# Top-k experts in two groups of two batches, the selection moved beside attention and beside the experts

## The chip, the cores and the metric

The kernel runs as one program on one core of a Trainium2 chip. A core has five engines with instruction queues of their own: TensorE (PE in the profile; its weight loads are PEld), VectorE (DVE), ScalarE (ACT), GpSimd (POOL) and SyncE (SP, which only issues transfers here). They meet through semaphores. The metric is the device time in microseconds of one execution. Before the change the median of three runs is 1038.39 us (1035.84 to 1040.92).

## The reference

Four batches of 512 tokens with 256 columns pass through two layers. Each layer is a cross attention and a mixture of experts, each added to the residual stream `x`. Only the second layer's mixture and the end of its attention are touched. Cut to that:

```
scores = einsum('ntd,de->nte', layernorm(x), gate_w)      # 4 x 512 x 8
probs  = softmax(scores).transpose(0, 2, 1)               # 4 x 8 x 512
g, m   = top_k(probs, 128)                                # per batch and expert
xin    = layernorm(x)[m]                                  # 4 x 8 x 128 x 256
h      = gelu(xin @ w1[e]) @ w2[e]                        # 256 -> 1024 -> 256
out    = zeros.at[m].add(g[..., None] * h)
x      = x + bfloat16(out)
```

Each expert takes the 128 best of the 512 tokens of every batch. A batch's selection needs that batch's final `x` alone, so it does not have to wait for the other batches. All data are float32.

## The kernel before

There are four stages, one block each: attention 0, a top-1 mixture, attention 1 and the top-k mixture (`moe_top_k`). A block's engines start together when the block before has ended on all of them.

**Attention** runs in 64 steps of two halves, 16 steps per batch, four per slot of four heads. The order of work is written out by `attention_schedule`. In step t TensorE computes the scores of step t (L703), the raw scores of step t + 8, whose row maxima DVE takes (`maxima`, L920), and the products with the values of step t - 1 (L722); ACT takes the exp (L846). So the last maxima are taken at step 55. Scores and raw scores share a ring of three PSUM units: a unit is written again only after its reader is done. Smaller jobs hang on step numbers and share one PSUM bank, `misc`: the transpose of the maxima ("m"), the head outputs ("o"), the transposed output ("at") and the output projection ("a"), whose result DVE adds to `x` (L911). Batch b's last addition comes 21 steps after the start of its 16, at 16b + 21. Steps from 64 on only finish jobs, and TensorE runs six dummy calls ahead of each (`keep_awake`, L632, two matmuls per call).

At step 57 DVE normalises the first three batches (`normalise`, L93 to L101), and at steps 60 to 62 TensorE transposes them (`turn_normalised`, L110) and DVE copies them to `xnt` (L124).

**moe_top_k.** DVE normalises batch 3. TensorE computes the gate products of all batches (L133). DVE and ACT make softmax weights, and TensorE turns them so that each of 64 partitions holds one (batch, expert, half of the tokens) with 256 candidates. Sixteen rounds on DVE take 8 maxima, find their positions and strike them out (L1630 to L1633), which sorts each half's best 128. TensorE turns the result, and DVE keeps the better of the k-th best of one half and the k-th worst chosen of the other (L1641 to L1645): the token table and the weights `gate_w`. POOL gathers rows of the normalised tokens from memory by the table (`gather`, L1494).

Then eight experts follow, each for the 4 x 128 = 512 chosen tokens of all batches. Per expert TensorE computes 8 hidden blocks of 48 matmuls in all, 512 columns wide (L1591), turns the next expert's tokens (L1575), and computes 4 x 24 output matmuls, 256 wide (L1604). Products are made of parts: high x high, low x high and high x low. ACT casts the weights to the high part (`weights_high`, L1526), and DVE subtracts to get the low part (`weights_low`, L1658) from `wf`, which has a single buffer; `wr`, with the parts, has two. SP may load a half of `wf` again only when its low part is made (`weight_low_ready`). ACT computes each hidden block's gelu twice (L1534, L1537), DVE makes the hidden low part (L1672), and DVE weights the outputs (L1666). POOL adds them into `acc` in memory (`scatter`, L1503). At the end SP loads `acc` (L1477), DVE adds it to `x`, and SP stores `out` (L1480).

## Time and profile before

| what | us |
|---|---|
| median of three runs | 1038.39 |
| the profiled execution, as timed | 1033.42 |
| its span from first to last instruction | 1031.6 |
| attention 1 ends on DVE | 768.8 |
| first expert matmul | 829.04 |
| last expert matmul ends | 1014.8 |
| PE busy in the span | 933.5 (90%) |
| DVE busy | 611.2 (59%) |
| ACT busy | 501.6 (49%) |
| POOL busy | 308.2 (30%) |

Times of rows are counted from the span's start. A busy TensorE is not a useful TensorE: the dummy matmuls of `keep_awake` count as busy.

### The profile page before, as it was taken

To read this page: it belongs to the slowest core of one execution; us is meant where nothing else is said; L and a number is where in the kernel's file an instruction comes from. 1 tells how busy PE (TensorE), PEld (TensorE's weight loads), DVE (VectorE), ACT (ScalarE), POOL (GpSimd) and SP (SyncE) were. 2 spreads that over 40 slices of the span, in tenths; PEclk is the share of its full clock that TensorE was granted. 3 is DMA by queue.
4 is the path that set the end of the run, shared out by engine and by line. 5 is a ranking of instruction groups with operands and counts; after the bars stand their busy time and mean duration, and the time that the engine had idled before them with its cause. 6 is when DMAs were issued, how large, how long until landed. Compare 5 with 4: busy or idle time off the path is not lost. (4 is left out here: it accounts for less than half of the span.)

```text
span 1031.6 us, 17287 instructions
## 1 busy us (share of the span) xinstructions
PE 933.5 (90%) x6782; PEld 639.1 (62%) x6782; DVE 611.2 (59%) x1052; ACT 501.6 (49%) x753; POOL 308.2 (30%) x295
## 2 busy tenths in 40 slices
PE   3389999998889999998889989999999989999993
PEld 3134444443759999997634444444489989999993
DVE  7588989996331111113887858787735565565553
ACT  1148887776042323232347857667622044555550
POOL 7697662000012222223304022000003245444222
PEclk9559999999599999999859999999997999999997
DMA  7877665301489999994735161600107125544316
GB/s 261 172 218 193 134 159 101 60 4 64 156 313 420 373 331 336 347 334 130 190 89 134 35 124 34 121 9 4 64 21 248 37 81 154 152 129 124 102 21 184
DMA packets 53045, 158.97 MB, mean 154 GB/s; under 512 B 8272, under 2 KB 28368, under 8 KB 42288
## 3 DMA queue, kind: packets, MB, share of 16 engines
q1 hardware_dynamic: 36464, 121.96, 39.5%
q0 software_dynamic: 13296, 29.63, 11.0%
q10 hardware_dynamic: 3216, 6.43, 1.7%
q8 instruction: 47, 0.77, 0.3%
q14 instruction: 22, 0.18, 0.1%
HBM read 116.18 MB, written 40.76 MB: 152 GB/s over the span
## 5 line engine op out<-in xcount | busy, mean ns | idle before, releaser
L920 DVE TENSOR_REDUCE a_row_max<-ps_ring 128x2 f32<-128x1024 f32 x256 | 308.3, 1221 | 70.6 <-PE ps_ring L688 69.7
L846 ACT ACTIVATE a_probs<-ps_ring 128x1024 f32<-128x1024 f32 x256 | 261.3, 1024 | 98.5 <-PE ps_ring L703 96.1
L722 PE MATMUL ps_out<-a_probs,a_vaug 128*32 128x256 f32 x2048 | 166.1, 397 | 1.5 <-ACT a_out_sb L852 1.0
L688 PE MATMUL ps_ring<-a_ka,a_qa 52*128 52x512 f32 (+1 forms) x512 | 124.1, 487 | 30.5 <-DMA a_ka<-scratch_k_scr 20.1
L703 PE MATMUL ps_ring<-a_qa,a_ka 56*128 56x512 f32 (+1 forms) x512 | 131.2, 509 | 1.4 <-DVE a_row_max L920 1.3
L1187 ACT ACTIVATE e_hid<-ps_ring,e_wts 128x128 f32<-128x128 f32 x184 | 52.1, 371 | 115.1 <-DMA e_wts<-in_w 52.8
L703 PEld LDWEIGHTS ps_ring<-a_qa,a_ka 56*128 56x128 f32 (+1 forms) x512 | 48.8, 187 | 94.6 <-issue 67.0
L1534 ACT ACTIVATE e_hr<-ps_ring 128x512 fp32r<-128x512 f32 x64 | 38.3, 599 | 120.5 <-PE ps_ring L1591 78.7
L688 PEld LDWEIGHTS ps_ring<-a_ka,a_qa 52*128 52x128 f32 (+1 forms) x512 | 52.5, 203 | 66.4 <-ACT a_probs L846 23.0
L1591 PE MATMUL ps_ring<-e_xt,e_wr 128*128 128x512 f32 x384 | 88.7, 390 | 2.3 <-DVE e_xt L1652 2.3
L722 PEld LDWEIGHTS ps_out<-a_probs,a_vaug 128*32 128x32 f32 x2048 | 40.9, 108 | 77.0 <-issue 74.6
L1275 PEld LDWEIGHTS ps_ring<-e_xst,e_wts 128*128 128x128 f32 x736 | 85.7, 192 | 1.9 <-issue 0.8
L1275 PE MATMUL ps_ring<-e_xst,e_wts 128*128 128x128 f32 x736 | 86.0, 275 | 0.6 <-DVE e_xst L1356 0.6
L1287 PE MATMUL ps_ring<-e_wts,e_hid 128*128 128x256 f32 x368 | 83.8, 381 | 1.1 <-ACT e_hid L1187 1.1
L1591 PEld LDWEIGHTS ps_ring<-e_xt,e_wr 128*128 128x128 f32 x384 | 71.6, 188 | 17.0 <-issue 2.4
L1672 DVE TENSOR_TENSOR e_hr<-e_hf,e_hr 128x512 fp32r<-128x512 f32 x64 | 44.4, 694 | 54.5 <-ACT e_hf L1537 51.6
L1287 PEld LDWEIGHTS ps_ring<-e_wts,e_hid 128*128 128x128 f32 x368 | 68.1, 190 | 10.7 <-ACT e_hid L1187 2.3
L1503 POOL DMA_INDIRECT scratch_acc<-e_ys,e_token x32 | 57.1, 1784 | 54.7 <-DVE e_ys L1666 50.8
L1134 POOL DMA_INDIRECT scratch_ys<-e_ys,e_to_row x23 | 22.8, 993 | 121.8 <-DVE e_ys L1365 121.8
L1494 POOL DMA_INDIRECT e_xg<-scratch_xl,e_token x32 | 32.3, 1009 | 78.0 <-PE ps_ring L1575 48.7
L1365 DVE TENSOR_TENSOR e_ys<-ps_ring,e_wts 128x256 f32<-128x256 f32 x23 | 9.8, 424 | 76.7 <-PE ps_ring L1287 76.7
L1362 DVE TENSOR_TENSOR e_xst<-ps_misc,rms_t 128x256 f32<-128x256 f32 x22 | 9.3, 424 | 73.9 <-PE ps_misc L1252 73.9
(234 smaller groups left out, 1252.9 us busy)
## 6 DMA issues: line engine op xcount, KB each, us to landing
e_wts<-in_w SPq DMA_DIRECT2D x23, 1156.0 KB
e_wts<-in_w SPq DMA_DIRECT2D x23, 1024.0 KB
e_wf<-in_w SPq DMA_DIRECT2D x16, 1024.0 KB, 6.7
a_qa<-scratch_q_scr SPq DMA_DIRECT2D x28, 384.0 KB, 8.7
a_ka<-scratch_k_scr SPq DMA_DIRECT2D x28, 384.0 KB, 7.2
scratch_q_scr<-a_qst POOLq DMA_DIRECT2D x36, 256.0 KB, 3.7
scratch_k_scr<-a_kst POOLq DMA_DIRECT2D x9, 512.0 KB, 11.8
scratch_q_scr<-a_qst SPq DMA_DIRECT2D x12, 256.0 KB, 3.3
```

Of the source, the lines that this page charges most:

```text
L688: ins = pe.matmul(to[:, par], qa[rows, b % 2, g, p, qt * P:(qt + 1) * P], ka[rows, b % 2, g, p], start=True, stop=True)
L703: ins = pe.matmul(to[:, par], ka[rows, b % 2, g, p, kc * P:(kc + 1) * P], qa[rows, b % 2, g, p], start=True, stop=True)
L722: ins = pe.matmul(m.ps_out[VW * h:VW * (h + 1), cols], vaug[:, b % NV, kc, HG * g + h], probs[:, t % 3, h, cols], start=(kc == 0 and half ...
L846: nc.scalar.activation(probs[:, t % 3, 2 * half:2 * half + 2], unit("s", n), ACT.Exp, scale=HD ** -0.5).then_inc(exp_done, 1)
L920: dve.tensor_reduce(row_max[:, s % 3, qt, :, p], unit("m", n), AX.X, ALU.max).then_inc(mx_read, 1)
L1187: nc.scalar.activation(hid[:, k, fc], m.ps_st[:, 2 * k + half, q * P:(q + 1) * P], ACT.Silu, bias=wts[:, k, w1_cols + FC * D + fc:w1_cols ...
L1275: ins = pe.matmul(m.ps_st[:, 2 * k + half, q * P:(q + 1) * P], wts[:, k, c * F + fc * P:c * F + (fc + 1) * P], xst[:, k, c], start=(c == 0 ...
L1287: ins = pe.matmul(m.ps_max[:, k, 0:D], hid[:, k, fc], wts[:, k, w1_cols + fc * D:w1_cols + (fc + 1) * D], start=(fc == 0), stop=(fc == FC ...
L1503: pool.indirect_dma_start(dram["acc"], bass.IndirectOffsetOnAxis(token[:, e, b:b + 1], 0), ys[:, e % 2, b], None, compute_op=ALU.add).then ...
L1534: nc.scalar.activation(hr[:, 0, fc], m.ps_st[:, fc % 4], ACT.Gelu_apprx_tanh)
L1591: ins = pe.matmul(m.ps_st[:, fc % 4], wr[:, k, wp, c * F + fc * P:c * F + (fc + 1) * P], xt[:, xp, c], start=(c == 0 and (wp, xp) == (0, 0 ...
L1672: dve.tensor_tensor(hr[:, 1, fc], hf[:, fc % 4], hr[:, 0, fc].bitcast(F32), ALU.subtract).then_inc(h_split, 1)
```

## The change

There are now two groups, batches 0 and 1 and batches 2 and 3. The 16 rounds of picks are done once per group (the partitions are 32 in place of 64, the free size is the same 256).

The first group's selection moves into attention 1. Batch 0 is normalised at step 37 and batch 1 at step 53, and their transposes follow one step later. Gate products come at step 57 (job "g"), the turned weights at 59 ("r"), pick rounds at steps 60 to 71 (`ROUNDS_AT`), and the token table at 73 and 74 ("p", "w"). The mixture's block normalises batches 2 and 3, and gathers at once. The second group's selection is spread over steps 0 to 6 of the experts (`ROUNDS_IN`).

The experts run twice, once per group: 16 steps i with 256 tokens each. Every expert's weights are therefore loaded, cast and split twice. The low part of the first weight half stays on DVE in one instruction (`first_low`), that of the second half moves to POOL (`second_low`). The first group's sums are loaded after the weights of step 11, added by DVE in steps 12 and 13 and stored after the weights of step 14.

```diff
-EARLY_AT = {(60, 1): ("x", 0), (61, 1): ("x", 1), (62, 1): ("x", 2)}
+EARLY_AT = ({(60, 1): ("x", 0), (61, 1): ("x", 1), (62, 1): ("x", 2)}, {(38, 1): ("x", 0), (54, 1): ("x", 1)})
+ROUNDS_AT = {60: (0, 2), 61: (2, 4), 62: (4, 6), 63: (6, 8), 65: (8, 10), 69: (10, 14), 71: (14, 16)}
+def pick(dve, chain, s, r):
+    cols = slice(8 * r, 8 * r + 8)
+    chain.link(dve.max(s.best[:, cols], s.rows[:, r % 2]))
+    chain.link(dve.max_index(s.best_at[:, cols], s.best[:, cols], s.rows[:, r % 2]))
+    if r < ROUNDS - 1:
+        chain.link(dve.match_replace(s.rows[:, (r + 1) % 2], s.best[:, cols], s.rows[:, r % 2], -1.0))
...
+        for kind, t in (("g", 57), ("r", 59), ("p", 73), ("w", 74)):
+            put((kind, 0), t, 0)
...
-                        if (t, half) == (56 + layer, 1):
...
+                        if layer == 1 and (t, half) in ((37, 1), (53, 1)):
+                            b = (t - 37) // 16
+                            dve.wait_ge(misc_free, index["a", b, 1] + 1)
+                            normalise(dve, chain, m, 1, b, b + 1)
+                        if layer == 1 and half == 0 and t in ROUNDS_AT:
+                            for r in range(*ROUNDS_AT[t]):
+                                pick(dve, chain, sel, r)
...
+        DONE_IN = E - 2
+        ROUNDS_IN = {1: (0, 2), 2: (2, 6), 3: (6, 10), 4: (10, 13), 5: (13, 16)}
...
+                for i in range(1, N):
                     for part in range(2):
-                        weight_low_ready(sp, part, e - 1)
-                        load_weights(e, part)
+                        sp.wait_ge(w_lo[part], i)
+                        load_weights(i, part)
+                    if i == E + 3:
+                        for k in range(2):
+                            sp.wait_ge(y_added[k], 16 * GB * (E // 2))
+                        for b in range(GB):
+                            load_sum(b)
+                    if i == E + 6:
+                        for b in range(GB):
+                            store_out(b)
...
+                def second_low(i):
+                    pool.wait_ge(w_hi[1], i + 1)
+                    pool.tensor_tensor(wr[:, i % 2, 1, HALF:], wf[:, HALF:], wr[:, i % 2, 0, HALF:].bitcast(F32), ALU.subtract).then_inc(w_lo[1], 1)
+                for i in range(N):
+                    if i + 2 < N:
+                        pool.wait_ge(x_full, i + 1)
+                        gather(i + 2)
+                    if i:
+                        scatter(i - 1)
+                    if i + 1 < N:
+                        second_low(i + 1)
...
-                keep_awake(34)
-                turn(0)
-                keep_awake(10)
+                keep_awake(60)
+                turn_tiles(GB)
+                turn(0)
...
+                    if i + 1 < N:
+                        split_x(i + 1)
+                        first_low(i + 1)
+                    weighted(i, 0)
...
+                    if i in ROUNDS_IN:
+                        for r in range(*ROUNDS_IN[i]):
+                            pick(dve, chain, sel, r)
...
+                    weighted(i, 1)
+                    if E + 4 <= i < E + 4 + GB:
+                        total(i - E - 4)
```

On DVE the norm came behind the last row maximum of attention 1. This is the end of the maxima before:

```order
L920 TENSOR_REDUCE a1_row_max<-ps_ring 128x2 x2
L926 TENSOR_SCALAR a1_neg_max<-a1_row_max 128x8x2
L927 SCALAR_TENSOR_TENSOR a1_neg_max<-a1_row_max,a1_neg_max 128x8x2
L891 RECIPROCAL a1_rden<-ps_misc 128x16
L898 TENSOR_TENSOR a1_att<-ps_misc,a1_rden 128x4x64
L911 TENSOR_TENSOR x_res<-ps_misc,x_res 128x512
L93 BN_STATS a1_stats<-x_res 128x6 x12
L96 BN_AGGR a1_mv<-a1_stats 128x2 x12
```

Now one batch's norm stands between maxima of step 53 and step 54 (the same stands at 37 and 38, for batch 0):

```order
L77 SCALAR_TENSOR_TENSOR a1_tmp1<-a1_tmp1,a1_tmp0 128x4
L78 SCALAR_TENSOR_TENSOR a1_rstd<-a1_tmp1,a1_rstd 128x4
L101 TENSOR_SCALAR a1_ctx_t<-x_res,a1_mv,a1_rstd 128x256 x4
L1029 TENSOR_REDUCE a1_row_max<-ps_ring 128x2 x2
L1020 TENSOR_TENSOR x_res<-ps_misc,x_res 128x512
L124 COPY xnt1<-ps_ring 128x1024
L1029 TENSOR_REDUCE a1_row_max<-ps_ring 128x2 x2
L1035 TENSOR_SCALAR a1_neg_max<-a1_row_max 128x8x2
```

L1029 is the row maximum (L920 before), L1020 the addition of the projected output (L911 before). Four maxima of steps 54 and 55, which came without a break before, now stand behind the norm, with a copy of the turned tiles between them.

On POOL, this is the expert loop before (L1494 gathers, L1503 scatters, L1489 is the low part of the first expert's weights):

```order
L1489 TENSOR_TENSOR e1_wr<-e1_wf,e1_wr 128x2048 x2
L1494 DMA e1_xg<-scratch_xl,e1_token 128x256 x16
L1503 DMA scratch_acc<-e1_ys,e1_token 2048x256 x4
L1494 DMA e1_xg<-scratch_xl,e1_token 128x256 x4
L1503 DMA scratch_acc<-e1_ys,e1_token 2048x256 x4
```

And now (L1613 gathers, L1623 scatters, L1629 is the low part of the second weight half):

```order
L1613 DMA e1_xg<-scratch_xl,token 128x256 x2
L1629 TENSOR_TENSOR e1_wr<-e1_wf,e1_wr 128x2048
L1613 DMA e1_xg<-scratch_xl,token 128x256 x2
L1623 DMA scratch_acc<-e1_ys,token 2048x256 x2
L1629 TENSOR_TENSOR e1_wr<-e1_wf,e1_wr 128x2048
L1613 DMA e1_xg<-scratch_xl,token 128x256 x2
```

The subtraction stands in every one of the 16 steps, behind that step's two scatters and ahead of the next two gathers.

On SP, the end of the last block before:

```order
L1460 DMA e_wf<-in_w 128x2048 x14
L1477 DMA e_xn<-scratch_acc 128x4x256 x4
L1480 DMA out_x<-x_res 128x4x256 x4
L1454 UNCONDITIONAL_BRANCH
```

And now:

```order
L1566 DMA e_wf<-in_w 128x2048 x22
L1570 DMA e_sums<-scratch_acc 128x4x256 x2
L1566 DMA e_wf<-in_w 128x2048 x6
L1575 DMA out_x<-x_res 128x4x256 x2
L1566 DMA e_wf<-in_w 128x2048 x2
L1570 DMA e_sums<-scratch_acc 128x4x256 x2
L1575 DMA out_x<-x_res 128x4x256 x2
```

Loads of weights are 30 behind the first two in place of 14, and sums and stores of the first group stand ahead of eight and two of them.

## Rows read from the trace of the kernel before

**Rows 1.** Chain in order of time; columns: start us, duration us, engine, tile, line.
```profile
769.28 6.94 PE ps_out L133 x48
...
788.73 0.43 DVE e_best L1630
...
790.22 0.43 DVE e_best L1630
...
829.04 11.15 PE ps_ring L1591 x48
...
841.06 2.88 PE ps_out L1604 x24
...
852.57 10.91 PE ps_ring L1591 x48
...
1015.59 4.60 DMA scratch_acc<-e_ys,e_token
1020.20 5.60 DMA e_xn<-scratch_acc
```

**Rows 2.** Timeline, last expert products on TensorE; start, duration, engine, line, operation.
```profile
1011.75 3.04 PE L1604 MATMUL ps_misc<-e_wr,e_hr 128*128 128x256 f32 x24
```

**Rows 3.** Timeline of DVE, end of attention and norm of batch 3.
```profile
768.12 0.69 DVE L911 TENSOR_TENSOR x_res<-ps_misc,x_res 128x512 f32<-128x512 f32 x1 [3.72 <-PE ps_misc L646]
769.14 1.41 DVE L93 BATCH_NORM_STATS2 e_stats<-x_res 128x6 f32<-128x256 f32 x4 [0.32 <-PEq L386]
...
773.38 1.38 DVE L101 TENSOR_SCALAR e_xn<-x_res,e_mv,e_rstd 128x256 f32<-128x256 f32 x4
```

**Rows 4.** Groups by line, 636 to 652; busy us, mean ns, idle before.
```profile
L920 DVE TENSOR_REDUCE a_row_max<-ps_ring 128x2 f32<-128x1024 f32 x12 | 14.6, 1221 | 1.7 <-PE ps_ring L688 1.7
```

**Rows 5.** Timeline of TensorE, starts of steps 56 and 60, dummies, a job.
```profile
726.95 0.51 PE L703 MATMUL ps_ring<-a_qa,a_ka 52*128 52x512 f32 x2
...
739.68 0.50 PE L703 MATMUL ps_ring<-a_qa,a_ka 52*128 52x512 f32 x2
...
755.55 1.50 PE L632 MATMUL ps_ring<-ident 128*128 128x128 f32 x12
756.89 0.60 PE L638 MATMUL ps_misc<-ident,a_att 128*128 128x128 f32 x4
```

**Rows 6.** Windows: length, busy PE, PEld, DVE, ACT, POOL, clock, DMA share, GB/s.
```profile
814.00:816.00 2.00, 2.00 (x12) 2.00 (x11) 0.57 (x4) 0.00 (x0) 1.03 (x1) 0.51 0.06 12
...
818.00:820.00 2.00, 2.00 (x21) 2.00 (x20) 0.00 (x0) 0.00 (x0) 1.52 (x2) 1.00 0.45 131
```

**Rows 7.** Groups by line and shape in the experts, 829 to 1012.
```profile
L1503 POOL DMA_INDIRECT scratch_acc<-e_ys,e_token x30 | 54.0, 1798 | 52.0 <-DVE e_ys L1666 48.2 <-issue 3.8
...
L1672 DVE TENSOR_TENSOR e_hr<-e_hf,e_hr 128x512 fp32r<-128x512 f32 x64 | 44.4, 694 | 54.5 <-ACT e_hf L1537 51.6 <-issue 2.9
...
L1658 DVE TENSOR_TENSOR e_wr<-e_wf,e_wr 128x1024 fp32r<-128x1024 f32 x28 | 33.4, 1214 | 0.0
L1526 ACT CAST e_wr<-e_wf 128x2048 fp32r<-128x2048 f32 x14 | 26.0, 1911 | 0.0
L1494 POOL DMA_INDIRECT e_xg<-scratch_xl,e_token x22 | 22.7, 1030 | 53.9 <-PE ps_ring L1575 48.7 <-issue 5.2
...
L1666 DVE TENSOR_SCALAR e_ys<-ps_out,e_gate_w 128x256 f32<-128x256 f32 x16 | 7.7, 481 | 3.5 <-PE ps_out L1604 3.5
```

**Rows 8.** The tile e_wf: POOL's subtractions (ns min/median/max), and landings of its loads.
```profile
L1489 POOL TENSOR_TENSOR e_wr<-e_wf,e_wr x2: 4526/4526/4527, 786.1 to 790.6; 128x2048 fp32r<-128x2048 f32 x2
...
DMA to landing us min/median/max: 5.2/6.7/8.1
```

**Rows 9.** Timeline of DVE, then of POOL, near the span's start.
```profile
11.86 0.68 DVE L362 TENSOR_TENSOR a_kf<-a_ctx_t,a_sin_t 128x512 f32<-128x512 f32 x1
12.58 1.64 DVE L363 TENSOR_TENSOR a_kf<-a_kf 128x512 f32<-128x512 f32 x1
...
12.23 1.44 POOL L374 TENSOR_TENSOR a_turn_a<-a_qx,a_cos_t 128x512 f32<-128x512 f32 x1 [6.35 <-ACT a_qx L785]
```

More of the change, by code:

```diff
@@ L258, in attention @@
             att_t = ctx_t[:, 3]
+            s1 = qx[:].rearrange("p j c t -> p (j c t)")
+            s2 = xn[:].rearrange("p j i d -> p (j i d)")
+            sel = Memory()
+            sel.rows = s1[0:ROWS, 0:T].rearrange("p (r t) -> p r t", r=2)
+            sel.best = s1[0:ROWS, T:T + CAP]
+            sel.best_at = s1[0:ROWS, T + CAP:T + 2 * CAP].bitcast(U32)
+            sel.best_tok = s1[0:ROWS, T + 2 * CAP:T + 3 * CAP]
+            sel.picks = s1[:, T + 3 * CAP:T + 3 * CAP + 2 * ROWS].rearrange("p (w h n) -> p w h n", w=2, h=2)
+            sel.prob = s2[:, 0:8 * E].rearrange("p (n e) -> p n e", e=E)
+            sel.work = s2[:, 8 * E:16 * E].rearrange("p (n e) -> p n e", e=E)
+            sel.prob_j = s2[:, 16 * E:24 * E].rearrange("p (j h b e) -> p j h b e", j=2, h=2, b=GB)
+            sel.top = s2[:, 24 * E:25 * E]
+            sel.first, sel.token_f = (s2[:, (26 + 2 * i) * E:(28 + 2 * i) * E] for i in range(2))
         ln = m.ln = Memory()
@@ L854, in _ @@
                             act_job(job)
+                        if layer == 1 and (t, half) == (58, 0):
+                            act.wait_ge(m.max_off, 1)
+                            nc.scalar.activation(sel.prob, sel.work, ACT.Exp).then_inc(m.exp_done, 1)
             @block.vector
@@ L1402, in moe_top_k @@
[L1402 to L1411 removed]
+        ln.stats = sb("stats", [P, NT, 6], F32)
@@ new lines, in moe_top_k @@
+        ln.mv = sb("mv", [P, NT, 2], F32)
+        ln.rstd = sb("rstd", [P, NT], F32)
+        ln.tmp = [sb(f"tmp{i}", [P, NT], F32) for i in range(2)]
+        sel = Memory()
+        sel.work = sb("work", [P, GT, E], F32)[:]
+        sel.prob = sb("prob", [P, GT, E], F32)[:]
+        sel.top = sb("top", [P, GT], F32)[:]
+        sel.prob_j = sb("prob_j", [P, 2, 2, GB, E], F32)[:]
+        sel.rows = sb("rows", [ROWS, 2, T // 2], F32)[:]
+        sel.best = sb("best", [ROWS, CAP], F32)[:]
+        sel.best_at = sb("best_at", [ROWS, CAP], U32)[:]
@@ L1496, in scatter @@
-                def scatter(e):
-                    if e:
-                        pool.wait_ge(y_added[1 - e % 2], 16 * B * ((e + 1) // 2))
-                    for b in range(B):
-                        pool.wait_ge(y_copied, B * e + b + 1)
-                        done = y_added[e % 2] if e < E - 1 else last_added[b]
-                        pool.indirect_dma_start(dram["acc"], bass.IndirectOffsetOnAxis(token[:, e, b:b + 1], 0), ys[:, e % 2, b], None,
-                                                compute_op=ALU.add).then_inc(done, 16)
@@ new lines, in scatter @@
+                def scatter(i):
+                    e, b0 = i % E, GB * (i // E)
+                    if e:
+                        pool.wait_ge(y_added[1 - i % 2], 16 * GB * ((i + 1) // 2))
+                    for b in range(GB):
+                        pool.wait_ge(y_copied, GB * i + b + 1)
+                        done = y_added[i % 2] if i < N - 1 else last_added[b]
+                        pool.indirect_dma_start(dram["acc"], bass.IndirectOffsetOnAxis(m.token[:, e, b0 + b:b0 + b + 1], 0), ys[:, i % 2, b], None,
+                                                compute_op=ALU.add).then_inc(done, 16)
@@ new lines, in _ @@
+                        if i == DONE_IN and fc == 6:
+                            pe.wait_ge(m.picks_ready, 5)
+                            for what in range(2):
+                                ins = pe.matmul(ps_sel[:, T // 2 + what * GB * E:T // 2 + (what + 1) * GB * E], m.turned[:], sel.picks[:, what, 1], start=True, stop=True)
+                            ins.then_inc(picks_turned, 1)
+                    if i == 1:
+                        pe.wait_ge(m.picks_ready, 3)
+                        for j in range(2):
+                            ins = pe.transpose(ps_sel[0:ROWS, T // 2 + j * P:T // 2 + (j + 1) * P], sel.prob_j[:, j].rearrange("p h b e -> p (h b e)"), m.ident[:])
+                        ins.then_inc(picks_turned, 1)
@@ L1695, in setup @@
+                for b in range(GB, B):
+                    total(b)
 def setup(nc, ctx, dram):
```

468 lines of the change are left out of this document (246 added, 222 removed).

## The prediction, made before the changed kernel ran

> **What bounds the kernel now.** I read the page's slices first: TensorE is busy nearly everywhere, so only the stretches where it does nothing useful can be shortened. The chain in order of time names the largest: DVE's last attention operation ends at 768.8 [rows 3], and the first expert's matmul starts at 829.04 [rows 1]. Between lie the fourth batch's norm, gate products at 769.28, sixteen pick rounds on DVE (788.73 to 812) and a gather. TensorE fills that time with dummy matmuls. From 829.04 the eight experts run back to back on TensorE, until its last products, begun at 1011.75, end at 1014.8 [rows 1, 2]. That is 185.7 us, 23.2 each. Then 16.8 us of scatter, reload, add and store follow; the chain's later pieces are a scatter's landing from 1015.59 and a reload from 1020.20 [rows 1].
>
> **The yardstick.** Sums are made on the profiled execution: 1031.6 us of span, 1033.4 us as timed. The three runs shown have a median of 1038.4, 5.0 above it; I add that at the end.
>
> **1. A norm in the middle of attention.** Before, three batches are normalised together at step 57, behind the last row maximum. Now batches 0 and 1 are normalised at steps 37 and 53, between maxima. One batch costs 5.6 us: it runs from 769.14 (BN_STATS) to the end of the last TENSOR_SCALAR at 774.76 [rows 3]. There DVE is nearly the bound: of 16 us it reduces 14.6 and waits 1.7 [rows 4]. TensorE shares a ring of three units with DVE and cannot get past unread maxima: at step 38 the new turn of the tiles needs both the norm and a read maximum, so the loss is nearly whole. The turn (1.1) and its copy (1.2) lie beside the stalled output products. I take 5.6 twice = 11.2. Bounds: 2 x 3.5 if DVE's waits give some back, 2 x 8 if turn and copy come on top.
>
> **2. The end of attention.** Step 56 begins at 726.95 and the rest ends at 768.8, after 41.9 [rows 3, 5]. New: 32 gate matmuls at step 57. The old 48 took 6.94, partly at half clock [rows 1]; I take 3.5. The three turns at 60 to 62 and their waits go (about 4.3). Then the picks: rounds are 1.49 apart (788.73 to 790.22) [rows 1], and 16 of them are 23.8 us on DVE alone. They start at 16.6: steps 56 to 59 took 12.7 (726.95 to 739.68) [rows 5], and the gates and the turned rows add 3.5 and 0.4. With two head outputs of 0.7, two output additions of 0.7 [rows 3], a wait of 0.9 for the last products and a token addition of 0.3 and semaphores, DVE is done at about 45; two small turns with dummy matmuls ahead of them (12 in 1.34, [rows 5]) and six small DVE operations make 49.0. So the stage ends 7.1 later. Bounds 4 to 11. The fourth group's outputs queue behind rounds on DVE here, and TensorE waits for them.
>
> **3. From attention to the first expert.** The next block starts at 769.1 + 11.2 + 7.1 + 1 (one dip of the clock after the low work of the gates, my estimate) = 788.4. DVE's norm of two batches takes about 8.5. TensorE first runs 60 dummy calls, 120 matmuls at the 12 in 1.34 of rows 5: 13.4; after a pause it will start at half clock for some 3.5 us, as from 814 until full clock is back by 818 [rows 6], which adds 1.7. Then two turns 1.5 and the split of x 1.4 (two operations on half the columns, against 2.5 now). Weights are ready earlier (load, 1.9 cast, 2.3 subtraction). So the first expert starts 18.0 after the block: 806.4 against 829.04, **22.6 gained**. The picks' 60 us have gone off the chain, but 37 of them return as terms 1 to 3.
>
> **4. Sixteen half experts in place of eight.** 24 matmuls of 256 columns take 2.88 [rows 1], 0.120 each. A half expert has 48 + 48 of them and four turns (0.44): 11.95. Sixteen are 191.2, minus the last's turn 0.4. Added to TensorE inside step 0: eight turns 1.0 and 32 gate matmuls 3.5. That is 195.3 with nothing waiting, already 9.6 over 185.7, since 512 columns took 10.91 per 48 and 256 take 5.76.
>
> *DVE.* Per step: 8 hidden subtractions at about 0.34 (0.694 for 512 columns), split 1.4, low half of the first weights 2.3 (1.214 for 1024 columns), two weightings 0.85 [rows 7]: about 7.2. Four pick rounds add 6.0, which is 13.2 against 11.95 in steps 2 and 3: 1.7 lost together, since four hidden banks absorb some. Steps 1, 4 and 5 just fit. In step 6 TensorE must wait for the last picks and again for the turned pairs: 2.9.
>
> *The second weight half.* It is no longer done by DVE but by POOL, in one 4.53 us instruction [rows 8], between 2 gathers (1.25 each with the gap) and 2 scatters (1.8 and 0.3, [rows 7]): 11.2 of 11.95 busy. More important is the loop through the single buffer e_wf: a load may be issued only when the subtraction of the half before has ended. Issue 0.3, landing, ACT's cast 1.9, POOL 4.53, semaphores 0.3 make 7.0 + landing. Landings are 5.2 / 6.7 / 8.1 [rows 8], the long ones when both halves are in flight 2.7 us apart. Now the halves are about 4 us apart, so I take 6.0: period 13.0. The loop starts with some 3 us of lead, and picks and step 6 give lead back, so it binds only in the second group: five steps x 1.0 = 5.0. Bounds: 0 at 4.9, +13 at the median 6.7.
>
> *Totals and stores.* SP now sends 2 loads of sums behind the weights of step 11 and 2 stores behind those of step 14, the second behind a DVE addition of step 13. Weight loads queue behind them, and with no spare buffer TensorE waits. I take 3 for SP.
>
> *DVE against POOL.* At 12.23 POOL's L374 ran 1.44 us, and DVE's L363, alone 0.68, took 1.64: it ended 0.55 after POOL's end [rows 9]. The two took turns by whole instructions. So DVE's subtractions of two SBUF tiles stand still while POOL's 4.53 us run, and the same for the addition of the totals. The four hidden banks hide most of it; the totals in steps 12 and 13 don't: 4.5. The Trainium skill, "SBUF — State Buffer", section "SBUF: two separate sides", says the same in general: the shared port pair is an exclusive lock held for the full instruction. By that rule, the stage is 4.5 longer than by adding durations, and the rows at 12 us agree with it; no row has a POOL instruction of this length beside a two-input DVE one.
>
> Stage: 195.3 + 1.7 + 2.9 + 5.0 + 3.0 + 4.5 = **212.4**, 26.7 more than 185.7.
>
> **5. The tail.** Two batches remain to be summed in place of four: the reload took 5.6 behind the others [rows 1], alone about 4.4. 1.2 gained.
>
> **Sum.** 1033.4 - 22.6 + 26.7 - 1.2 = 1036.3; with the 5.0 to the median, **1041 us**, 0.3% above before. A measurement of this kernel tells about 0.5%, 5.2 us, from no change.
>
> **Rivals.**
> *A, clean overlap (faster).* Landings near 5.2 with less in flight, lead lasting through the second group, the exclusive turns falling on idle time. Then the stage is 195.3 + 2.9 = 198.2, own time 1022.1, median 1027. For it: by these sums every engine but TensorE has idle time in a step. Against: POOL at 94% of 11.95 and a loop that closes only below 4.9 of landing; no landing was below 5.2.
>
> *B, the weight loop binds throughout (slower).* If the second halves land at 6.7, each step from the first few on takes 13.7, plus the sums and stores: about 221 for the stage, own time 1044.9, median 1050. At 8.1 it would be over 1060. It decides from the point where the landing exceeds 4.9. For it: the bytes of weights double (2 MB in 12 us instead of 23). Against: the two halves no longer compete.
>
> *C, attention hides the norm.* If DVE's waits absorb 4 of 11.2, 1037; by itself that is no change.
>
> *D, the change doesn't move picks off the chain.* The first group's picks begin only at step 60 and run past the attention's end; were the token table ready 5 later than in term 2, 1046.
>
> **How the numbers follow.** Forecast with C and D's smaller forms: 0.45 (of it 0.30 within 0.5%, 0.12 slower, 0.03 faster). A: 0.28, B: 0.27. Of B, 0.01 falls within 0.5%. So faster is 0.31, same 0.31, slower 0.38. The forecast's own range is 1035 to 1047; the 8-in-10 range reaches to A and past B's middle: 1026 to 1055.
>
> **What would show it.** Right: a 5 to 6 us hole in TensorE behind steps 37 and 53; block start near 788; first expert matmul near 806; steps of 12.0 in the first group except 2, 3 and 6, and 13 to 14 in the second with ACT waiting for e_wf; DVE's L1791 stretched beside POOL's 4.5 us. Wrong: steps of 12.0 to the end (A), steps of 13.7 from the third on (B), or DVE rounds that slow down beside POOL's subtraction, for which no term stands here.

## The result, and the profile after

The kernel after takes 1050.47 us (median of 4 runs, 1045.90 to 1052.84) against 1037.41 for the kernel before on the same chip (4 runs, 1035.84 to 1040.92). The ratio is 1.0139, 95% interval 1.0102 to 1.0176: slower by 1.3% where 0.3% was forecast. The profiled execution took 1049.03 us; its span is 1047.4 against 1031.6.

```profile
span 1047.4 us, 18129 instructions
PE 934.2 (89%) x7002; PEld 642.8 (61%) x7002; DVE 682.0 (65%) x1227; ACT 546.5 (52%) x900; POOL 380.2 (36%) x309
```

**Attention, after** (timeline: start, duration, engine, line, operation, and in brackets the idle time ahead with its releaser). These rows answer to [rows 3 to 5].

```profile
665.29 0.50 PE L789 MATMUL ps_ring<-a_qa,a_ka 52*128 52x512 f32 x2
670.47 1.97 PE L110 MATMUL ps_ring<-ident,a_ctx_t 128*128 128x128 f32 x8 [4.45 <-DVE a_row_max L1029]
675.49 0.69 DVE L1020 TENSOR_TENSOR x_res<-ps_misc,x_res 128x512 f32<-128x512 f32 x1 [3.95 <-PE ps_misc L705]
748.23 4.92 PE L133 MATMUL ps_misc<-gate,xnt 128*128 128x8 f32 x32
753.08 0.79 PE L789 MATMUL ps_ring<-a_qa,a_ka 52*128 52x512 f32 x2
753.80 1.08 PE L808 MATMUL ps_out<-a_probs,a_vaug 128*32 128x256 f32 x8
```

TensorE stands 4.45 us for the maxima that queue behind the first norm, turns the tiles in 1.97 instead of 1.09 (the eight turns before, at 745.43), and then DVE stands 3.95 for TensorE. The 32 gate matmuls take 4.92, and behind them a pair of scores takes 0.79, not 0.50. The stretches of that time (busy time and count of PE, PEld, DVE, ACT, POOL; then granted clock, DMA share, GB/s) go with it:

```profile
750.00:752.00 2.00, 2.00 (x14) 2.00 (x13) 0.00 (x0) 0.00 (x0) 0.00 (x0) 0.64 0.79 267
752.00:776.00 24.00, 23.87 (x134) 8.04 (x133) 13.39 (x50) 13.02 (x14) 0.00 (x0) 0.50 0.00 1
776.00:778.00 2.00, 2.00 (x14) 0.80 (x12) 0.00 (x0) 1.02 (x1) 0.00 (x0) 0.54 0.00 0
```

The granted clock is 0.50 (1.2 of 2.4 GHz) for 24 us and more, although TensorE is busy for 23.87 of 24.

**Experts, after** (the chain in order of time: start, duration, what), beside [rows 1]:

```profile
798.60 13.64 PE ps_ring L1676 x120
815.15 3.11 PE ps_ring L1709 x24
822.45 3.61 PE ps_ring L133 x32
...
912.11 4.60 POOL e_wr L1629
916.73 5.15 DMA e_wf<-in_w
...
924.40 4.62 DVE e_hr L1791
...
986.25 5.88 DVE e_half_b L1778
...
1006.71 8.00 DMA e_wf<-in_w
...
1019.01 8.03 PE ps_ring L1709 x48
...
1033.60 4.40 DMA scratch_acc<-e_ys,token
1038.01 3.99 DMA e_sums<-scratch_acc
```

The experts' block starts at 798.60, the first expert's products at 815.15, and the last products (begun 1029.76, 3.04 long) end at 1032.80. By the starts of TensorE's L1709, steps 0 to 14 last 18.1, 12.2, 12.0, 12.1, 13.2, 12.1, 14.1, 14.1, five times 12.57, 14.5 and 19.0 us; the last takes 13.8.

**The loop of the second group** (timeline, rows of one step; steps 8 to 12 repeat it):

```profile
947.82 6.01 PE L1709 MATMUL ps_ring<-e_xt,e_wr 128*128 128x256 f32 x48
948.07 0.48 DVE L1764 TENSOR_SCALAR e_ys<-ps_misc,gate_w 128x256 f32<-128x256 f32 x1
948.68 5.17 POOL L1629 TENSOR_TENSOR e_wr<-e_wf,e_wr 128x2048 fp32r<-128x2048 f32 x1
949.52 7.16 DVE L1791 TENSOR_TENSOR e_hr<-e_hf,e_hr 128x256 fp32r<-128x256 f32 x8 [0.97 <-ACT e_hf L1664]
...
956.66 1.62 POOL L1623 DMA_INDIRECT scratch_acc<-e_ys,token  x1 [0.30 <-issue]
...
958.04 2.29 DVE L1758 TENSOR_TENSOR e_wr<-e_wf,e_wr 128x2048 fp32r<-128x2048 f32 x1
958.58 3.18 POOL L1623 DMA_INDIRECT scratch_acc<-e_ys,token  x1 [0.30 <-issue]
958.90 1.91 ACT L1654 CAST e_wr<-e_wf 128x2048 fp32r<-128x2048 f32 x1 [0.89 <-DMA e_wf<-in_w]
960.25 0.48 DVE L1764 TENSOR_SCALAR e_ys<-ps_out,gate_w 128x256 f32<-128x256 f32 x1
960.64 0.48 DVE L1764 TENSOR_SCALAR e_ys<-ps_misc,gate_w 128x256 f32<-128x256 f32 x1
961.23 5.19 POOL L1629 TENSOR_TENSOR e_wr<-e_wf,e_wr 128x2048 fp32r<-128x2048 f32 x1
```

Two circles run here, and a reader can take either for the cause. One is the forecast's: POOL's end at 953.86, load and landing, ACT's cast to 960.81, POOL again. It does not close quite in time: POOL starts 0.42 behind the cast, where in the first group it starts 0.07 behind it, so by itself this circle needs about 12.2 (5.04 to the cast's start, 1.91, 0.07, 5.17; an estimate from these rows). The other takes the whole 12.57. DVE's hidden subtraction is held from 949.52 until POOL's 5.17 us are over. DVE then needs 6.5 for seven more hidden subtractions, the split and L1758, which ends at 960.33. POOL's second scatter lies over L1758: its row is 3.18 long, not 1.6 (the end is rough: it overlaps the next row by 0.5), and POOL's next subtraction, which stands behind it in the queue, starts 0.9 after L1758's end. 5.17 + 7.4 = 12.57. POOL is never idle in this loop (subtraction, two gathers, two scatters, gaps of 0.2 to 0.3). Its scatters wait for no weighting of this step: when the two of this step start, 18 and 19 had started before them, and DVE had done 20 weightings by 948.6, so their inputs are those of the step before.

### The profile page after: what moved, and what is told of

It is laid out like the page before. It is cut to its first block and busy times, and to the rows that moved or that the text cites. A ratio compares the mean times of both kernels' runs of the same rounds, so it can differ in the third digit from the quotient of the medians.

```text
span 1047.4 us, 18129 instructions
## 1 busy us (share of the span) xinstructions
PE 934.2 (89%) x7002; PEld 642.8 (61%) x7002; DVE 682.0 (65%) x1227; ACT 546.5 (52%) x900; POOL 380.2 (36%) x309
## 5 line engine op out<-in xcount | busy, mean ns | idle before, releaser
L1029 DVE TENSOR_REDUCE a_row_max<-ps_ring 128x2 f32<-128x1024 f32 x256 | 308.1, 1221 | 67.3 <-PE ps_ring L774 66.2
L808 PE MATMUL ps_out<-a_probs,a_vaug 128*32 128x256 f32 x2048 | 172.4, 411 | 0.9 <-ACT a_out_sb L938 0.6
L789 PE MATMUL ps_ring<-a_qa,a_ka 56*128 56x512 f32 (+1 forms) x512 | 134.7, 523 | 2.7 <-DVE a_row_max L1029 1.3
L1306 ACT ACTIVATE e_hid<-ps_ring,e_wts 128x128 f32<-128x128 f32 x184 | 51.9, 372 | 115.2 <-PE ps_ring L1394 60.5
L1709 PE MATMUL ps_ring<-e_xt,e_wr 128*128 128x256 f32 x768 | 98.5, 288 | 8.6 <-DVE e_wr L1758 6.3
L1613 POOL DMA_INDIRECT e_xg<-scratch_xl,token x32 | 34.3, 1070 | 188.9 <-POOLq L439 176.3
L1709 PEld LDWEIGHTS ps_ring<-e_xt,e_wr 128*128 128x128 f32 x768 | 95.2, 195 | 10.8 <-DVE e_wr L1758 8.8
L1629 POOL TENSOR_TENSOR e_wr<-e_wf,e_wr 128x2048 fp32r<-128x2048 f32 x16 | 78.9, 4930 | 39.5 <-ACT e_wr L1654 39.5
L1791 DVE TENSOR_TENSOR e_hr<-e_hf,e_hr 128x256 fp32r<-128x256 f32 x128 | 77.4, 651 | 16.1 <-ACT e_hf L1664 15.0
L1654 ACT CAST e_wr<-e_wf 128x2048 fp32r<-128x2048 f32 x32 | 60.9, 1928 | 34.9 <-DMA e_wf<-in_w 34.9
L1661 ACT ACTIVATE e_hr<-ps_ring 128x256 fp32r<-128x256 f32 x128 | 49.8, 389 | 32.4 <-PE ps_ring L1709 28.0
L1623 POOL DMA_INDIRECT scratch_acc<-e_ys,token x32 | 60.5, 1890 | 13.2 <-issue 8.6
## 6 DMA issues: line engine op xcount, KB each, us to landing
scratch_k_scr<-a_kst POOLq DMA_DIRECT2D x9, 512.0 KB, 13.2
```

The costliest lines, as they stand in the source:

```text
L789: ins = pe.matmul(to[:, par], ka[rows, b % 2, g, p, kc * P:(kc + 1) * P], qa[rows, b % 2, g, p], start=True, stop=True)
L808: ins = pe.matmul(m.ps_out[VW * h:VW * (h + 1), cols], vaug[:, b % NV, kc, HG * g + h], probs[:, t % 3, h, cols], start=(kc == 0 and half ...
L1029: dve.tensor_reduce(row_max[:, s % 3, qt, :, p], unit("m", n), AX.X, ALU.max).then_inc(mx_read, 1)
L1623: pool.indirect_dma_start(dram["acc"], bass.IndirectOffsetOnAxis(m.token[:, e, b0 + b:b0 + b + 1], 0), ys[:, i % 2, b], None, compute_op=A ...
L1629: pool.tensor_tensor(wr[:, i % 2, 1, HALF:], wf[:, HALF:], wr[:, i % 2, 0, HALF:].bitcast(F32), ALU.subtract).then_inc(w_lo[1], 1)
L1654: nc.scalar.copy(wr[:, i % 2, 0, cols], wf[:, cols]).then_inc(w_hi[part], 1)
```

## The experiments

All start from the kernel after unless said. Because the start of the layer differs from execution to execution (the last turn of maxima ahead of the first norm, behind the same instructions, lay between 657.1 and 669.0), each profile is read by four stretches, in us: **mid**, from that turn (659.13 before, 657.10 after) to the fifth turn after it, the first behind the second norm (732.20, 746.71); **end**, from there to the experts' block; **first**, from the block to the first expert's products; **rest**, to the end of the span. The ratio is to the kernel before as it ran beside each kernel (medians of 1035.3 to 1038.1), so it compares better than the medians. The rest holds step 0, which lasted 16.4 to 19.5 as a dip of the clock fell into it or not, whatever the edit; differences of rest under 3 us are read with that in mind.

| kernel | mid | end | first | rest | median us | ratio to before |
|---|---|---|---|---|---|---|
| before | 73.1 | 36.9 | 59.9 | 202.6 | 1037.4 | |
| after | 89.6 | 51.9 | 16.6 | 232.3 | 1050.5 | 1.014 |
| gate dummies, 12 calls | 90.1 | 47.1 | 16.6 | 231.6 | 1052.1 | 1.015 |
| turn dummies, 36 calls | 95.6 | 53.1 | 16.6 | 230.8 | 1056.5 | 1.016 |
| turn dummies, 14 calls | 87.3 | 46.9 | 16.6 | 231.9 | one run | |
| norms late | 73.0 | 57.8 | 18.6 | 234.1 | 1047.9 | 1.011 |
| POOL in quarters | 89.3 | 48.4 | 16.6 | 236.3 | 1055.0 | 1.017 |
| two buffers | 90.2 | 48.3 | 16.6 | 232.5 | 1050.7 | 1.013 |
| two buffers, POOL ahead of scatters | 89.0 | 53.0 | 16.6 | 230.0 | 1047.8 | 1.012 |
| DVE subtracts in group two | 89.4 | 48.4 | 16.6 | 224.3 | 1042.5 | 1.008 |
| totals late | 89.5 | 48.5 | 16.5 | 228.4 | 1046.0 | 1.009 |
| all, norms mid, 6 calls | 89.3 | 55.0 | 16.6 | 215.7 | 1038.2 | 0.999 |
| all, norms mid, 12 calls | 89.4 | 51.8 | 16.6 | 215.9 | 1035.7 | 0.996 |
| all, norms late | 73.0 | 56.8 | 18.6 | 216.9 | 1028.4 | 0.989 |

### Norms back behind the last maxima

```diff
-... {(38, 1): ("x", 0), (54, 1): ("x", 1)})
+... {(60, 1): ("x", 0), (61, 1): ("x", 1)})
-ROUNDS_AT = {60: (0, 2), 61: (2, 4), ... 71: (14, 16)}
+ROUNDS_AT = {65: (0, 5), 69: (5, 11), 71: (11, 16)}
-  (("g", 57), ("r", 59), ...
+  (("g", 62), ("r", 64), ...
-  (t, half) in ((37, 1), (53, 1)): ... normalise(dve, chain, m, 1, b, b + 1)
+  (t, half) == (57, 1): ... normalise(dve, chain, m, 1, 0, 2)
```

> The norms of batches 0 and 1 go back behind the last row maximum (step 57), the turns to steps 60 and 61, the gates to 62, the pick rounds to 65 to 71; the stores of the normalised tiles follow. The rest is the kernel after. Theory (the two norms among the maxima cost 16.5 us: 8.2 each, norm 5.6, copy 1.2, and the wait of DVE for a TensorE at half clock): the stretch between the turn of the maxima of slot 12's neighbour (before: 659.13 to 732.20, 73.1 us; after 89.6) falls back to about 73; behind it 16 rounds begin some 13 us later, so the block of the experts starts 65 us behind the last turned maxima in place of 51.9; net 3 us less, time about 1047. Rival (the loss in the middle is a different run's jitter or the gate constants): the stretch stays at 85 or more, time 1060.

Mid fell to 73.0, the value of before: the two norms are the whole 16.5. The price behind it was 5.9 in end, not 13, and 2.0 in first (the dummies start at half clock again: 15.69 for 120 in place of 13.64). Rest was 1.8 longer, 1.4 of it in step 0. The stretches gain 6.9 in sum; the medians differ by 2.6 and the runs scatter from 1042 to 1054, so the total alone shows less.

### Dummies in the two waits for the norm

```diff
+                        if layer == 1:
+                            full_size(36)     # 14 in the second kernel; into the free half of ps_misc
                         turn_normalised(pe, m, n, take_unit(kind, n))
```

> 36 dummy matmuls (4.0 us at full clock) are put into each of TensorE's two 4.45 us waits for DVE's norm, at steps 38 and 54; nothing else changes. Theory (the norm costs 16.5 us in attention in place of the forecast 11.2 because the clock falls to 0.50 in these waits, and TensorE then runs its turns and the residual product at half clock while DVE waits 3.95 for it): the clock stays at 1.00, each norm costs about 6 instead of 8.2, 2 us saved twice, time about 1046.5. Rival (DVE's own extra work, norm 5.6 plus copy 1.2, is the whole price and the clock only fills idle time): gain under 1 us, time 1050.

A miss in sizing: one dummy call is two matmul records of 0.112, so 36 calls ran 8.3 us where 4.45 were free, and mid grew by 6.0.

> Again dummies in TensorE's two waits for the norm (steps 38 and 54), the rest as after; each dummy call is two matmul records of 0.112, so 36 calls were 8.3 us, twice the wait; now 14 calls, 3.1 us of the 4.45. Theory (part of the 16.5 us is the clock that falls in the wait): the clock stays at 1.00 and the stretch from the last turned maxima ahead of the first norm to those behind the second shrinks from 89.6 to about 86. Rival (DVE's own work alone): it stays at 89 to 90.

Mid fell by 2.3. At the second norm the clock held at 1.00, and the two waits, 4.45 and 3.95 at the first norm of after, were these:

```profile
739.10 1.09 PE L110 MATMUL ps_ring<-ident,a_ctx_t 128*128 128x128 f32 x8 [1.13 <-DVE a_row_max L1037]
741.86 0.69 DVE L1028 TENSOR_TENSOR x_res<-ps_misc,x_res 128x512 f32<-128x512 f32 x1 [1.68 <-PE ps_misc L705]
```

That crossing took 25.3 from turned maxima to turned maxima, against 18.9 before and 26.9 after: 6.4 is the price of a norm at full clock, 1.6 the clock's. At the first norm the clock was already down ahead of the wait (rows from 668), and there only 0.8 came back:

```profile
668.00:672.00 4.00, 4.00 (x28) 1.35 (x24) 3.15 (x6) 2.06 (x3) 0.00 (x0) 0.50 0.98 184
```

### Dummies with the gate products

```diff
                     gate_products(pe, m, 0, ...).then_inc(m.logits_full, 1)
+                    full_size(6)
-                    return gate_products(pe, m, 1, ...)
+                    gate_products(pe, m, 1, ...)
+                    return full_size(6)
```

> Twelve dummy matmuls of 128 columns go between and behind the 32 gate matmuls of step 57; nothing else changes. In the kernel after, the granted clock falls from 1.00 to 0.50 behind the gates (about 751) and stays there until 777, so each half of steps 57 to 63 takes 1.73 us on TensorE instead of about 1.04. Theory (the thin gate matmuls of 8 columns drop the clock, and it is not given back while attention steps go on): with the dummies the clock stays at or near 1.00, the six halves of 57 to 59 save 4.1, then DVE's pick rounds (1.475 each) become the bound, so that of the rest only the idle 2.4 ahead of the fourteenth head output goes in part; the dummies cost 1.3. Block start 798.6 to about 793, time about 1045. Rival (attention steps without maxima are themselves too thin, whatever stands ahead of them): the clock falls a few us later all the same, gain under 1.5 us, time 1049 to 1051.

In this profile the clock held:

```profile
758.00:780.00 22.00, 19.78 (x189) 9.46 (x189) 14.66 (x55) 14.29 (x16) 0.00 (x0) 1.00 0.01 2
```

End was 47.1 instead of 51.9, the dummies included. But the four runs had a median of 1052.1, no less than after, and the kernels that leave this code alone show why one profile can't carry the theory: behind the same gates the spell at 0.50 lasted 10.2 us in four profiles (POOL in quarters, two buffers, DVE subtracts, totals late; end 48.3 to 48.5), 6.8 in one, and 27 to 31 in three (after; turn dummies 36; POOL ahead of scatters; end 51.9 to 53.1). So a long spell costs the stage 3.5 to 4.7 more than one of 10.2 us. With 6.8 us and no dummies end was 46.9, still 3 above the 44.0 that term 2 makes without its 1 for the clock. The last run asked again, on top of all other edits:

> The kernel with all edits and the norms among the maxima, with twelve dummy calls at the gates in place of six. In the profiles so far the spell of clock 0.50 behind the gates lasted 10.2 us four times and 27 to 31 us four times; with twelve calls (once) there was none, with six (once) 30.7. Theory (twelve calls hold the clock, and a long spell costs the stage some 5 us): no spell in the profile, gates to the experts' block 45.6 in place of 53.5 (six calls) or 50.4 (kernel after), median about 1033 against the 1038.2 with six. Rival (the one profile without a spell was chance): a spell of 10 or 30 us again, median 1037 to 1039.

With twelve calls the spell was there again, 10.2 us long (with six, 30.7). The theory that these dummies hold the clock has fallen; the one profile without a spell was chance, or needs something that wasn't isolated. The two medians, 1035.7 and 1038.2, differ in the direction of the shorter spell. The calls have a price too: with a spell of 10.2 us end was 51.8 with twelve of them, and 48.4 in the four kernels without.

### POOL's subtraction in quarters

```diff
-   pool.tensor_tensor(wr[:, i % 2, 1, HALF:], wf[:, HALF:], ..., ALU.subtract).then_inc(w_lo[1], 1)
+   for q in range(4):
+       cols = slice(HALF + q * HALF // 4, HALF + (q + 1) * HALF // 4)
+       ins = pool.tensor_tensor(wr[:, i % 2, 1, cols], wf[:, cols], ..., ALU.subtract)
+   ins.then_inc(w_lo[1], 1)
```

> POOL's subtraction of the second weight half, one instruction over 2048 columns (mean 4.93 us), becomes four over 512 columns; same work, same waits. Theory L (the period of 12.57 us in the second group is the loop through the one buffer: issue and landing 5.07, cast 1.91, 0.37, subtraction 5.18): the loop's sum does not shrink, DVE's hidden subtraction is held for at most 1.3 us instead of 4.6, but the period stays at 12.5 or grows since POOL's pieces now alternate with DVE's; time 1049 to 1053. Rival T (DVE held for a whole POOL instruction sets the period): with pieces DVE is through 3 us earlier, the period falls to about 12.0 and the totals' steps shrink; 0.6 times 6 and about 3 for the totals, time about 1044.

The period rose to 12.98, rest by 4.0 (1.4 of it in step 0, by a longer dip of the clock), and the median of 1055.0 lies above both forecasts; the rival's 12.0 has fallen:

```profile
944.34 5.59 POOL L1631 TENSOR_TENSOR e_wr<-e_wf,e_wr 128x512 fp32r<-128x512 f32 x4
945.18 7.57 DVE L1794 TENSOR_TENSOR e_hr<-e_hf,e_hr 128x256 fp32r<-128x256 f32 x8 [0.98 <-ACT e_hf L1667]
```

POOL's work grew from 5.17 to 5.59, and 5.59 + 7.4 = 12.99: the period follows POOL's time plus DVE's. The load loop gives nearly the same if the 0.37 to 0.42 between cast and POOL's start is counted to it (5.07 + 1.91 + 0.37 + 5.59 = 12.94), so the period of this run doesn't tell the two apart.

### A second buffer for the second weight half

```diff
-        wf = sb("wf", [P, 2 * HALF], F32)
+        wf = sb("wf", [P, 3 * HALF], F32)      # the second half of expert i lies in place 1 + i % 2
-                        sp.wait_ge(w_lo[part], i)
-                        load_weights(i, part)
+                        if i + part < N:
+                            sp.wait_ge(w_lo[part], i)
+                            load_weights(i + part, part)
```

> The second half of the weights gets two buffers in turn instead of one, so its load is issued a whole step ahead; POOL's single 2048-column instruction stays. Theory L (weight loop): landing 5.07 leaves the loop, ACT no longer waits for e_wf, steps 7 to 15 fall from 12.57 (14.05 in step 7) to 12.0 to 12.2, and TensorE's 1.28 wait in step 7 goes; 0.5 times 8 plus 2 in step 7 plus some of the last step's 8.0 landing, time about 1043. Rival T (DVE held behind POOL): the period stays near 12.5, time 1048 to 1050.

ACT no longer waits for e_wf, and the steady steps don't change: periods of 12.57, steps 6 and 7 at 14.1, rest 232.5.

```profile
948.54 5.17 POOL L1636 TENSOR_TENSOR e_wr<-e_wf,e_wr 128x2048 fp32r<-128x2048 f32 x1
955.90 3.75 ACT L1662 CAST e_wr<-e_wf 128x2048 fp32r<-128x2048 f32 x2
960.50 0.47 DVE L1772 TENSOR_SCALAR e_ys<-ps_misc,gate_w 128x256 f32<-128x256 f32 x1
961.09 5.19 POOL L1636 TENSOR_TENSOR e_wr<-e_wf,e_wr 128x2048 fp32r<-128x2048 f32 x1
```

ACT's two casts now run in one piece and end at 959.65, yet POOL starts at 961.09, 1.4 later, 0.12 after DVE's last weighting and behind its own stretched scatter (958.44, 3.18). The weight loop isn't what holds the period at 12.57.

### POOL's subtraction ahead of the scatters

```diff
+                    if i + 1 < N:
+                        second_low(i + 1)
                     if i:
                         scatter(i - 1)
-                    if i + 1 < N:
-                        second_low(i + 1)
```

> On top of the two buffers of the run before, POOL subtracts the next second weight half ahead of the scatters of the step before, not behind them, so it no longer waits for DVE's last weighting. Theory (serial loop of POOL's 5.17 and DVE's 7.4): POOL starts when ACT's second cast ends, 1.4 us earlier, and the period of the second group falls from 12.57 to between 12.0 and 12.3; about 3 us less than with the two buffers alone, time 1047. Rival (DVE is blocked as long wherever POOL's instruction stands): period 12.57, time 1050.

With this on top of two buffers the steps 7 to 12 fell to 11.95 to 11.96:

```profile
947.46 1.99 POOL L1620 DMA_INDIRECT e_xg<-scratch_xl,token  x1 [0.30 <-issue]
949.47 4.63 POOL L1636 TENSOR_TENSOR e_wr<-e_wf,e_wr 128x2048 fp32r<-128x2048 f32 x1
951.33 5.60 DVE L1799 TENSOR_TENSOR e_hr<-e_hf,e_hr 128x256 fp32r<-128x256 f32 x8 [0.93 <-ACT e_hf L1672]
961.45 4.63 POOL L1636 TENSOR_TENSOR e_wr<-e_wf,e_wr 128x2048 fp32r<-128x2048 f32 x1
```

So the queue order was the link that closed the circle, but not by the reason given ahead of the run. The scatters never waited for DVE's last weighting, and POOL did not start when ACT's cast ended (960.05) but 1.4 later, now behind a gather that lies over L1766 (1.97 to 1.99 long, 1.01 the one before it). What changed is the place in the step: POOL starts 0.24 ahead of TensorE's first expert product (949.71) where it started 0.86 behind it, its row is 4.63 and not 5.17, and DVE, which comes to its hidden subtraction at 951.33, is held for about 3 us in place of 4.6. Rest fell only by 2.4 against the two buffers alone: step 6 became 16.6, and 1.5 of the gain is step 0's clock. The new order with a single buffer was not run; by the estimate of 12.2 above, the weight loop could then bind a little.

### DVE subtracts in the second group

```diff
-                    if i + 1 < N:
+                    if i + 1 < E:
                         second_low(i + 1)      # POOL
...
                     weighted(i, 0)
+                    if E <= i + 1 < N:
+                        dve.wait_ge(w_hi[1], i + 2)
+                        dve.tensor_tensor(wr[:, (i + 1) % 2, 1, HALF:], wf[:, HALF:], ..., ALU.subtract).then_inc(w_lo[1], 1)
```

> For the second group's experts DVE subtracts the second weight half (2.29 us for 2048 columns), between the two weightings; POOL does it only in the first group. The two-buffer run took the landing out of the weight loop and the period stayed at 12.57, so the loop through the single buffer alone does not explain it. Theory (a serial loop of POOL's subtraction 5.17, in which DVE's subtraction of two SBUF tiles stands still, and DVE's whole work of a step 7.4, behind whose last weighting POOL's queue holds the next subtraction): without POOL's instruction DVE has 9.7 of work in a step, TensorE's 12.0 binds, and the weight loop is 5.07 + 1.91 + 2.6 = 9.6: steps 7 to 11 fall to 12.0, step 12's and 13's totals lose their blocked 5.9 and 4.3; 2 + 6 times 0.57 + 3 = 8 less, time about 1042. Rival (landing and ACT's casts bind the step whatever engine subtracts): period 12.4 or more, time 1048.

Rest fell by 8.0, and the median of 1042.5 is the one forecast; steps 8 to 13 last 11.95 to 11.96, step 7 15.5 and step 14 16.1. POOL's 5.2 became 2.3 on DVE, and the total's cast, 5.88 and 4.26 us in the chain of after, is

```profile
998.58 0.68 DVE L1778 CAST e_half_b<-e_sums 128x1024 bf16<-128x1024 f32 x1
...
1013.01 7.27 PE L1709 MATMUL ps_ring<-e_xt,e_wr 128*128 128x256 f32 x46 [4.02 <-DVE e_wr L1758]
```

The 4.02 in front of the last step stay: they are SyncE's store ahead of the last weights.

### Totals and stores of the first group behind the last expert

```diff
-  if i == E + 3: ... load_sum(b)
-  if i == E + 6: ... store_out(b)
-  if E + 4 <= i < E + 4 + GB: total(i - E - 4)
+  (all four sums loaded, added and stored behind the last scatter)
```

> The first group's sums are loaded, added and stored behind the last expert again, together with the second group's; nothing is sent or added in steps 11 to 14. Theory (of the 8.4 us that steps 13 and 14 last above the period of 12.57, 1.9 are the addition on DVE between two steps and 6.5 SyncE's store, behind which the last expert's weights were issued at 1006.7 and landed 8.0 later): both go, TensorE's last wait of 6.3 and the dip of its clock with it; the tail grows by 1.5 to 2.5 for four sums in place of two; time about 1043.5. Rival (early sums are free and the tail gains from them): steps 13 and 14 stay long for want of weights, time 1052.

Steps 11 to 14 last 12.57 each. The last step starts 195.5 behind the first instead of 203.9, and from there to the end it takes 4.5 more: 3.9 net, so the median of 1046.0 is above the 1043.5 expected. The part behind the last product alone grew by 5.0 (14.6 to 19.6) where 1.5 to 2.5 was expected. So early sums pay, and the store stood in the wrong place. The kernels with all edits keep the sums where they are and send the stores behind the last expert's weights (`if i == N - 1`); the last step then starts 11.95 after the one before.

### All edits together

DVE in POOL's place from the expert of step 7 on, stores behind the last weights, six dummy calls at the gates; norms late or mid.

> Four edits of the runs before together: norms of batches 0 and 1 behind the last maxima; DVE in POOL's place for the second weight half from the expert step 7 on; the first group's stores sent behind the last expert's weights; six dummy calls (twelve matmuls) between and behind the gate matmuls. Theory (the loss is made of these parts, and they add): from the last turned maxima ahead of the first norm to the first expert 149.3 as in the run with late norms, less 3 for a clock that stays up = 146.5; from there to the end 224.3 as in the run with DVE's subtraction, less 4.1 (the last step's wait for the stores) and 1.5 (step 7) = 218.7 (before the change: 169.9 and 202.6, together 7.3 more); time about 1028, ratio to before 0.993. Rival (the gains overlap: with one wait gone the next takes its place): 1033 to 1038, no difference from before.

> The same as the run beside it, but the norms of batches 0 and 1 stay among the maxima, as in the kernel after. Theory: the stretch to the first expert is 154 (158 in the kernel after, less 4 for the clock), the rest 218.7, together 7.5 more than in the run beside it; time about 1035, ratio 1.00. Rival (picks that begin late cost the other kernel as much as the norms in the middle cost this one): both within 2 us.

Late norms: 1028.39 (6 runs, 1023.84 to 1033.26), before 1038.09, ratio 0.9893, interval 0.9861 to 0.9924: faster than both kernels (that the gates' dummies have a share in it is not shown), and the sums of stretches (148.4 + 216.9) are the 365.2 forecast, its parts off by 1.9 in opposite directions. From step 7 to the last every step takes 11.94 to 11.96:

```profile
988.15 5.92 PE L1717 MATMUL ps_ring<-e_xt,e_wr 128*128 128x256 f32 x48
...
1000.11 5.92 PE L1717 MATMUL ps_ring<-e_xt,e_wr 128*128 128x256 f32 x48
```

Mid norms: 1038.21 (12 runs, 1029.33 to 1042.44), ratio 0.9986 (0.9965 to 1.0006), no difference from before. The ratio is the one expected, the time 3 above it: up to the first expert the profile took 160.9 where 154 was expected, with a spell of 30.7 us at 0.50 behind the gates, and the rest 215.7 where 218.7 was. The rival, both kernels within 2 us, has fallen.

## Why the prediction was off, step by step

The direction (slower) and the reasons of most steps held, and the measured median lies inside the range given but outside the forecast's own. On the profiled executions, forecast against measured:

| term | forecast | measured |
|---|---|---|
| start of the layer | 0 | -2.0 |
| 1 norms in mid attention | +11.2 | +16.5 |
| 2 end of attention, clock dip | +8.1 | +15.0 |
| 3 block to first expert | 18.0 | 16.6 |
| 4 the sixteen half experts | 212.4 | 217.6 |
| 5 tail | -1.2 | -2.2 |
| own time | 1036.3 | 1049.2 (timed 1049.03) |

**Term 1** has the right mechanism and place. Mis-sized: DVE's share is 6.4 per norm (forecast 5.6; turn and copy are not wholly beside the output products), and the clock, which had no term here, takes another 1.6 at the second norm and about 2 at the first (27.8 from turn to turn against 19.2 before, less 6.4).

**Term 2** failed in size twice. The gates took 4.92, not 3.5. "One dip of the clock, 1" was a spell of 27 us in this profile; with 10.2 us the stretch is 3.5 shorter, with 6.8 us 5.0 shorter. And even then (46.9) the stretch is 3 longer than summed: the rounds start 17.4 after step 56's turn of maxima (746.71 to 764.14) where 11.4 was summed (16.6 from the step's start, 5.2 ahead of that turn), DVE waiting 2.93 for ACT's exponential, 3.02 for the turned rows and 2.44 for the head output, where small operations had been counted and not the places in the schedule at which they stand. In steps 60 to 63 DVE was not the bound: it idles 2.44 for TensorE behind its eighth round.

**Term 3** was 1.4 too long: TensorE came into the block at full clock, so the dummies took 13.6. With late norms it was 18.6.

**Term 4.** Step 0 was 1.7 longer than summed, for a dip of the clock behind its gates. Picks in steps 2 to 5 lost 1.5, nearly all in step 4 (forecast 1.7). Step 6: 2.1 (2.9). *The weight loop* is the step that failed in substance. It was priced 5.0 at a landing of 6.0; the halves landed in about 5.1, which by the same sum (7.0 + 5.1 = 12.1) is 0.15 a step, and taking the landing out altogether gained nothing. What bound was the exclusive turns of DVE and POOL, forecast as hidden by the four hidden banks except at the totals. They aren't hidden: one blocked subtraction puts DVE's whole list behind POOL's instruction, and at the list's end L1758 lies over POOL's scatter, behind which the next subtraction stands in the queue: 0.62 in each of five steps. The forecast had POOL's queue as 11.2 of 11.95, with every instruction at its length alone; beside DVE it filled the 12.57; and POOL's instruction is 5.17, not 4.53. Step 7 (2.1) is the same kind: POOL's L1629 comes at 911.6, behind gathers and scatters of step 6. *Totals and stores* were 7.5; steps 13 and 14 took 8.4 above the period, of which SyncE's store ahead of the last weights is most (the wait ahead of the last step is 6.30) and the blocked cast 1.9. The last step added 2.2 by the clock, which fell in that wait (8.03 for the 48, not 5.77).

The turns themselves held: POOL's end releases DVE within 0.3 us. The Trainium skill, "SBUF — State Buffer", section "SBUF: two separate sides", names a second case that the forecast passed over: a copy from SBUF to SBUF in a fast mode of DVE takes the same lock, and holds up GpSimd's writing of descriptors. The total's cast, an SBUF copy, was held in this way behind POOL's subtraction (5.88 against 0.68 alone); no run isolates its being in a fast mode. For the descriptors, a scatter on POOL took 3.18 where it lay over DVE's L1758 and 1.62 elsewhere, and a gather 1.97 over the same operation in place of 1.01. L1758 is no copy but a subtraction of two SBUF inputs, and only adjacency is shown.

**Rivals.** B's number, 1050, is the one measured, by another mechanism: no landing of a second half was the bound in the steady steps, as two buffers show. A was excluded by the 12.57. C went the other way: attention hides none of the norm. D had the right sign: the first group's table was ready 7 later than forecast, up to 5 of it for want of clock (by the profile with 6.8 us at half clock). That the total came within 1% is no proof of the sum: only terms 3 and 5 and the start were shorter, by 4.4 together, and terms 1, 2 and 4 missed by 17.4 the other way.

## What to carry to other kernels

Two circles with nearly equal period look alike in a profile; take the link out of each in turn (a buffer for one, the order in a queue for the other) before believing either, and look whether an instruction starts at once when the circle in question lets it. When work moves to an engine that shares a port with a busy one, add the two engines' times instead of taking the larger, and look at what stands behind the blocked instruction in both queues. A SyncE store that waits for a late result must stand behind the loads that the next step needs, and work on the engine that nearly binds a stage belongs behind that stage: with POOL's subtraction on DVE in the second group, the stores behind the last weights and the norms behind the maxima (and six dummy calls, whose worth is not shown), the same idea runs 1.1% faster than before.

## What was not expected of the hardware

- The granted clock stayed at 0.50 while TensorE was busy for 23.87 of 24 us. Behind the same 32 matmuls of 8 columns the spell lasted 27 to 31 us in three profiles, 10.2 in four, 6.8 in one. The Trainium skill, "TensorE: Matmul & The Clock Gate", section "What's actually happening", says that the clock follows how busy the engine has been; by that rule so busy a stretch should have brought it back, and here it didn't. What sets the length stays open; dummies of full size at the gates did not settle it.
- Cutting POOL's 2048 columns into four instructions made it slower in all (5.17 to 5.59) and freed nothing.
- POOL's subtraction took 4.54 and 4.57 in the first and last step of after, where it met little of DVE, and 5.17 in the steps of the loop: its own length grew by 0.6 beside DVE.
